# Expert weights of 18 of 25 row tiles carried in the scattered rows and applied in ScalarE's copy of an expert tile's result

## What the reference computes

```python
tokens = patches @ W.T + b;  h = concat(class, tokens * pos, txt)      # [16, 193, 128]
h = h + linear_attention(layernorm(h)) + depthwise_conv3(layernorm(h))
xt = layernorm(h)
_, idx = top_k(xt @ gate_w.T + biases, 2)          # which two experts
topv, _ = top_k(xt @ gate_w.T, 2)                  # the two best raw scores
p = sigmoid(topv);  p = p / p.sum(-1, keepdims=True)
y[e] = (silu(xt @ w1[e]) * (xt @ w3[e])) @ w2[e]   # for the chosen e
out = h + p[0] * y[idx[0]] + p[1] * y[idx[1]] + shared(xt)
```

## Time and profile before

| | us |
|---|---|
| median of 3 runs | 252.32 (251.96 to 253.23) |
| the profiled execution: its own time, its span | 254.19, 252.3 |
| busy in the span: PE, DVE, ACT, POOL | 223.3, 190.1, 155.8, 114.7 |

### The profile page before, as it was taken

The page is one execution under the profiler, slowest core; times in us unless marked ns, Lnnn a source line. Parts: engine busy times, 40 slices in busy tenths (PEclk is TensorE's granted clock), DMA queues, the critical chain, the costliest instruction groups (busy, mean ns, idle before and its releaser), DMA issues.

```text
span 252.3 us, 5578 instructions
## 1 busy us (share of the span) xinstructions
PE 223.3 (89%) x1477; PEld 191.5 (76%) x1485; DVE 190.1 (75%) x741; ACT 155.8 (62%) x438; POOL 114.7 (45%) x122
## 2 busy tenths in 40 slices
PE   3888879999899999988989979999999999999930
PEld 2768779989798989766576657888888888887720
DVE  3548896999999999988986778666666666665892
ACT  3056575676876867849863266666666666666390
POOL 1400000084837483803667703666666666666400
PEclk9999995999999999979999999999999999999995
DMA  6999981060607010100113331423332232329666
GB/s 189 353 360 355 328 315 62 0 232 26 233 24 243 22 56 22 42 10 13 55 42 93 79 83 34 115 62 100 92 89 81 84 94 83 90 81 275 159 157 190
DMA packets 31565, 31.68 MB, mean 126 GB/s; under 512 B 4338, under 2 KB 27419, under 8 KB 30768
## 3 DMA queue, kind: packets, MB, share of 16 engines
q1 hardware_dynamic: 27240, 24.57, 32.5%
q0 software_dynamic: 3392, 6.36, 7.7%
q10 hardware_dynamic: 904, 0.41, 0.6%
HBM read 22.80 MB, written 9.03 MB: 126 GB/s over the span
## 4 chain that ended last, share of the span: by engine, by line
PE 60%; DVE 24%; ACT 6%; issue 4%; DMA 2%; SPq 1%; DVEq 0%; ACTq 0%
PE bank L1621 15%; PE bank L1641 10%; PE bank L1630 5%; PE bank L1539 3%; PE bank L1333 3%; PE bank L1524 3%; PE bank L1527 3%; DMA cst<-in_consts 2%; DVE st L842 2%; PE bank L1610 2%; PE bank L1402 2%; PE bank L1416 2%; DVE sh_h L1103 2%; DVE att L908 2%; DVE att L899 2%
## 5 line engine op out<-in xcount | busy, mean ns | idle before, releaser
L813 POOL DMA_INDIRECT xs_dram<-xd,pos_i x50 | 55.4, 1109 | 69.7 <-DVE pos_i L1002 56.9
L824 POOL DMA_INDIRECT y_dram<-att,goal x56 | 55.1, 985 | 37.3 <-ACT att L749 37.0
L1333 PE MATMUL bank<-wt,xp_both 128*128 128x128 f32 x288 | 39.6, 290 | 5.7 <-DMA xp_both<-in_patches 5.4
L1333 PEld LDWEIGHTS bank<-wt,xp_both 128*128 128x128 f32 x288 | 37.3, 202 | 7.3 <-DMA xp_both<-in_patches 5.9
L735 ACT ACTIVATE att<-bank 128x256 f32<-128x256 f32 x56 | 21.5, 384 | 24.4 <-PE bank L1621 24.0
L1240 DVE CAST xsT_h<-bank 128x128 fp32r<-128x128 f32 x56 | 16.3, 291 | 24.4 <-PE bank L1610 24.4
L1641 PE MATMUL bank<-w_sb,att 128*128 x224 | 34.7, 277 | 0.0
L1641 PEld LDWEIGHTS bank<-w_sb,att 128*128 128x128 f32 x224 | 29.4, 191 | 0.5 <-issue 0.2
L1621 PE MATMUL bank<-xp_both,xsT_h 128*128 x56 | 26.8, 479 | 0.8 <-DVE xsT_l L1242 0.8
L1253 DVE TENSOR_TENSOR att<-att,bank 128x256 f32<-128x256 f32 x56 | 23.0, 411 | 1.7 <-ACT att L735 1.7
L1621 PE MATMUL bank<-xp_both,xsT_l 128*128 x56 | 22.2, 396 | 0.0
(11 more groups left out here) (212 smaller groups left out, 498.7 us busy)
## 6 DMA issues: line engine op xcount, KB each, us to landing
xp_both<-in_patches SPq DMA_DIRECT2D x6, 1152.0 KB
xs_all<-xs_dram SPq DMA_DIRECT2D x56, 64.5 KB, 1.8
xd<-y_dram SPq DMA_DIRECT2D x8, 384.0 KB, 4.8
w<-in_w SPq DMA_DIRECT2D x2, 1024.0 KB, 11.3
y_dram<-att,goal POOLq DMA_INDIRECT x56, 2.3
xs_dram<-xd,pos_i POOLq DMA_INDIRECT x50
xp_both<-in_patches SPq DMA_DIRECT2D x1, 768.0 KB, 5.6
hrow<-in_txt SPq DMA_DIRECT2D x2, 384.0 KB, 6.9
```

The lines of the kernel that those rows point to most:

```text
L813: nc.gpsimd.indirect_dma_start(out=xs_dram[:, :], out_offset=bass.IndirectOffsetOnAxis(ap=pos_i[0:rows, j, k:k + 1], axis=0), in_=xd[0:row ...
L824: nc.gpsimd.indirect_dma_start(out=y_dram[:, :], out_offset=bass.IndirectOffsetOnAxis(ap=goal[u][:, 0:1].bitcast(I32), axis=0), in_=ys[u][ ...
L1333: M(ps[:, 0:D], xp[p][:, k, :], wt[:, k, :], start=(k == 0), stop=False)
```

## The change

For the groups 0 to 5 (EARLIER = 6, the tiles below FROM = 18) the weight of each copy is computed before the scatter and travels as a second word of the row (ROW = 130 instead of 129 floats). `positions` no longer sorts these tokens' positions; copy k is choice k. POOL puts the sort into the goal instead (`goals`: it adds or subtracts the size of a half where the first choice is the higher expert), and computes the weights (`shares`: ten POOL operations for a group with `goals`, eight of them followed by a wait for the operation itself, which `pool_chain` counts). ACT gives the exponentials (`chances`), waiting for POOL's `shares` of the group before. ACT's copy of an expert tile's result multiplies by the word. Tiles 18 to 24 (LATE = 7 of them) keep the old way, with word 1.0. In the tail DVE adds chunks 0 to 2 as they are, ACT multiplies tiles 18 to 23 of both halves (`late_results`), and the order of DVE's tail is another.

```diff
-                nc.scalar.copy(ys[buf][:], bank[6 + q][:, 0:D]).then_inc(ys_done[at], 1)
+                A(ys[buf][:], bank[6 + q][:, 0:D], ACT.Copy, scale=goal[buf][:, 1:2]).then_inc(ys_done[at], 1)
...
+            def chances(g):
+                act.wait_ge(both_done, g + 1)
+                after(act, pool_chain, WEIGHED * g)
+                A(odds[:], raw8[:, 3 * g:3 * g + 3, 0:2], ACT.Exp, scale=-1.0).then_inc(odds_done, 1)
...
                 by_turns(i)
+                if i >= 2:
+                    chances(i - 2)
                 exps_rest(i)
...
+            def goals(g):
+                at = slice(3 * g, 3 * g + 3)
+                pool.wait_ge(both_done, g + 1)
+                then_pool(nc.gpsimd.tensor_copy(chosen[:], ix8[:, at, 0:2]))
+                then_pool(nc.gpsimd.tensor_tensor(crossed[:], chosen[:, :, 0], chosen[:, :, 1], ALU.subtract))
+                then_pool(nc.gpsimd.tensor_scalar(apart[:], crossed[:], 0.0, float(NID), ALU.is_gt, ALU.mult))
+                nc.gpsimd.tensor_tensor(xd[:, at, 0, D].bitcast(I32), ids[:, at, 0], apart[:], ALU.add)
+                nc.gpsimd.tensor_tensor(xd[:, at, 1, D].bitcast(I32), ids[:, at, 1], apart[:], ALU.subtract)
+            def shares(g):
+                at = slice(3 * g, 3 * g + 3)
+                pool.wait_ge(odds_done, g + 1)
+                then_pool(nc.gpsimd.tensor_scalar(odds[:], odds[:], 1.0, None, ALU.add))
+                then_pool(nc.gpsimd.tensor_tensor(odds[:], odds[:], minus[:].rearrange("p (t k) -> p t k", k=2), ALU.pow))
+                then_pool(nc.gpsimd.tensor_tensor(odds_sum[:], odds[:, :, 0], odds[:, :, 1], ALU.add))
+                then_pool(nc.gpsimd.tensor_tensor(odds_sum[:], odds_sum[:], minus[:, 0:3], ALU.pow))
+                then_pool(nc.gpsimd.tensor_tensor(xd[:, at, :, D + 1], odds[:], odds_sum[:].rearrange(
+                    "p (t o) -> p t o", o=1).broadcast_to([P, 3, 2]), ALU.mult))
             for g in range(G):
+                if g < EARLIER:
+                    goals(g)
+                    shares(g)
...
-                V.tensor_reduce(pos_2[:, a:b, :], prod[:, a:b], AX.X, ALU.add).then_inc(slots_done, 1)
-                dve.wait_ge(slots_done, g + 1)
-                    V.tensor_reduce(pos_i[:, a:b, 0], pos_2[:, a:b, :], AX.X, ALU.min)
-                    V.tensor_reduce(pos_i[:, a:b, 1], pos_2[:, a:b, :], AX.X, ALU.max).then_inc(pos_done, 1)
+                    if g < EARLIER:
+                        V.tensor_reduce(pos_i[:, a:b, :], prod[:, a:b], AX.X, ALU.add).then_inc(pos_done, 1)
...
-            then(V.tensor_tensor(swap[:], ix8[:, :, 0], ix8[:, :, 1], ALU.is_gt))
-            dve.wait_ge(raw_done, J)
+            then(V.tensor_tensor(swap[:], ix8[:, FROM:, 0], ix8[:, FROM:, 1], ALU.is_gt))
...
+            def add_results(c, k):
+                dve.wait_ge(y_loaded[k][c], 16)
...
+                    if b == CLS:
+                        dve.wait_ge(scaled, k + 1)
+                    last = V.tensor_tensor(hrow[:, a:b, :], hrow[:, a:b, :], y_rows[:, k, a:b, :], ALU.add)
```

More of the change, by code:

```diff
@@ L35 @@
 NID = J * P
+EARLIER = G - 2
+FROM = 3 * EARLIER
+LATE = J - FROM
 CAP = 3328
+WEIGHED = 8
 TILES = (2 * NTOK - E) // P + E
-ROW = D + 1
+ROW = D + 2
 BIG = 1 << 20
@@ L672, in _ @@
             rstd2(G - 2)
+            chances(G - 3)
             key_sums(G - 1)
@@ L759, in _, with late_results @@
             expert_steps(act, act_step, 2)
-            def second_results(c):
-                a = CHUNKS[c][0]
-                act.wait_ge(y_loaded[1][c], 16)
-                for j in range(a, weighed_by_act(c)):
-                    last = A(y_rows[:, 1, j, :], y_rows[:, 1, j, :], ACT.Copy, scale=weight[:, 1, j:j + 1])
+            def late_results(k):
+                c = len(CHUNKS) - 2
+                act.wait_ge(y_loaded[k][c], 16)
+                for j in range(FROM, CLS):
+                    last = A(y_rows[:, k, j, :], y_rows[:, k, j, :], ACT.Copy, scale=weight[:, k, j - FROM:j - FROM + 1])
                 last.then_inc(scaled, 1)
@@ L770, in _ @@
             shared_silu(EARLY + 1, 0)
+            late_results(0)
             shared_silu(EARLY + 1, 1)
-            second_results(0)
             shared_silu(EARLY + 2, 0)
             shared_silu(EARLY + 2, 1)
-            second_results(1)
-            for c in range(2, len(CHUNKS) - 1):
-                second_results(c)
+            late_results(1)
             for turn, c in list(enumerate(FINISHED))[2:]:
@@ L958, in raw_best @@
                 for j in tiles_of(g):
[L959 removed]
+                    V.max(raw8[:, j, :], sc[:, j, :])
             def choices(g):
@@ L1263, in _ @@
             expert_steps(dve, dve_step, 2)
-            def first_results(c):
+            def add_results(c, k):
                 a, b = CHUNKS[c]
                 rows = rows_of(a)
-                dve.wait_ge(y_loaded[0][c], 16)
-                for j in range(a, b):
+                dve.wait_ge(y_loaded[k][c], 16)
+                if k == 1:
+                    dve.wait_ge(fin_first, c + 1)
+                if a == CLS:
                     last = V.scalar_tensor_tensor(
-                        out=hrow[0:rows, j, :], in0=y_rows[0:rows, 0, j, :], scalar=weight[0:rows, 0, j:j + 1],
-                        in1=hrow[0:rows, j, :], op0=ALU.mult, op1=ALU.add)
-                last.then_inc(fin_first, 1)
@@ L1276, in all_results @@
-            def all_results(c):
-                a, b = CHUNKS[c]
-                m = weighed_by_act(c)
-                rows = rows_of(a)
-                dve.wait_ge(fin_first, c + 1)
-                dve.wait_ge(y_loaded[1][c], 16)
-                for j in range(m, b):
-                    last = V.scalar_tensor_tensor(
-                        out=hrow[0:rows, j, :], in0=y_rows[0:rows, 1, j, :], scalar=weight[0:rows, 1, j:j + 1],
-                        in1=hrow[0:rows, j, :], op0=ALU.mult, op1=ALU.add)
-                if m > a:
-                    dve.wait_ge(scaled, c + 1)
-                    last = V.tensor_tensor(hrow[:, a:m, :], hrow[:, a:m, :], y_rows[:, 1, a:m, :], ALU.add)
-                last.then_inc(fin_done, 1)
+                        out=hrow[0:rows, CLS, :], in0=y_rows[0:rows, k, CLS, :], scalar=weight[0:rows, k, CLS - FROM:LATE],
@@ L1292, in _ @@
+                        in1=hrow[0:rows, CLS, :], op0=ALU.mult, op1=ALU.add)
+                else:
+                    if b == CLS:
+                        dve.wait_ge(scaled, k + 1)
+                    last = V.tensor_tensor(hrow[:, a:b, :], hrow[:, a:b, :], y_rows[:, k, a:b, :], ALU.add)
+                last.then_inc(fin_done if k else fin_first, 1)
             dve.wait_ge(weight_done, 1)
             dve.wait_ge(sh_add, EARLY)
-            first_results(0)
-            first_results(1)
+            add_results(0, 0)
```

74 lines of the change are left out of this document (45 added, 29 removed).

## The result

The changed kernel takes 257.24 us (median of 4 runs, 256.76 to 258.37), the kernel before 252.60 beside it (251.96 to 253.23). The ratio is 1.019 with a 95% interval of 1.0146 to 1.0234. The prediction, 251.3 us with a range of 249.6 to 252.9, was wrong: the time lies 4.3 us above the upper end.

A forecast was written before the change was run, and what follows sets the result against it. PE bounds the kernel (60% of the chain); DVE's work counts only where PE waits. Loop -1.05, hits +0.4, ordering -0.2, tail -0.2 give -1.05 us: from 252.32 to 251.3 us, range 249.6 to 252.9.

The forecast's parts named there:

- the price of `goals` and `shares`: POOL, ahead of six groups' scatters: ten operations take 2.8 us (0 to 5.8), covered by 3.67 us of idle time.
- a scatter that starts a few us late costs nothing by itself: POOL's scatters: no engine waits before the first expert tile; idle times of 9.75 and 2.30 us precede groups 5 and 6.
- rival (3): ACT waits for POOL at `chances` from some 5.4 us a group on: some 254 us; chance 0.05.
- clock rival: TensorE's lowered clock at 107 to 117 us: shifted work escapes it, 1.7 us won, 249.6 us; chance 0.07.
- The loop: Attention loop: shorter `positions` lets DVE's turn start 0.25 us earlier in four iterations, 0.05 in a fifth: 1.05 us gained.
- ScalarE's exponentials and scaled copies: ACT: exponentials of some 0.2 us hide in a 0.7 us loop wait; scaled copies fit ACT's free time in the experts.
- The ordering by slot: DVE behind the loop: five operations shrink to 7 or 14 columns while PE idles 0.45 us; 0.2 us gained.
- The tail: Output end: first chunk's add ends at 242.7 instead of 242.88, SP's 7.59 us of issues follow; 0.2 us gained.
- the first `TENSOR_TENSOR`'s load of code: POOL's start: one code load, up to 8 us less the ten operations free; at about 6 us POOL starts some 1 us late.
- The 0.4 us for hits on DVE: Loop: POOL's operations beside DVE's turns delay DVE by one hit of 0.1 us in four iterations, 0.4 us lost.
- rival (2): POOL's work beside all three turns: three hits of 0.22 us in five iterations, 254.2 us; chance 0.08.
- rival (1): POOL's work fits ahead of DVE's turns in the loop, so 0.4 us is not lost: 250.9 us; chance 0.26.

The follow-up runs named there:

- goals only: Kernel before plus five POOL goal operations, first six groups unsorted on DVE, weights and tail as before: 253.52 us; second run 251.41 us.
- no powers: Changed kernel with POOL's two powers per group replaced by multiplications over the same tiles, so weights are wrong: 250.19 us, ratio 0.993.
- one power: Changed kernel with the same weights from one power instead of two, nine POOL operations per group: 250.87 us, ratio 0.990.
- before with ten operations: Kernel before plus the ten POOL operations per group for six groups, on tiles nobody reads: 256.69 us, ratio 1.019.

## Why the prediction was wrong

**The step that failed** is the price of `goals` and `shares`: "I take 2.8, ten copies end to end, since operands of 3 to 6 columns are smaller still and the waits make up for it". Measured were 5.5 us, beside the upper bound of 5.8 that the same paragraph gives, and 0.55 us an operation, which the prediction itself named as a sign of being wrong. The count of operations and waits was priced rightly (2.61 us with multiplications); that two of the ten are powers was not priced at all. A copy says nothing of a power: 1.37 us for six columns, 0.86 for three when nothing runs beside it. With these the ten take 4.46 us, as in group 5, which lies behind the loop. The rest, 1.0 us a group on average, is POOL held up: 0.1 by a wait for ScalarE in group 0, and 0.9 by VectorE, as shown below under the hits. Over groups 1 to 4 that is 5.2 us (5.76 + 6.61 + 5.09 + 5.57 less 4 x 4.46), as much as TensorE's added wait. So the powers' own time may not have been enough: (4.46 - 3.1) x 6 = 8 us is an estimate that stays inside the idle time of 12. No run has powers without the hold-ups, so how the two share the loss is not shown; without the powers there are neither.

**The step that hid it**: "a scatter that starts a few us late costs nothing by itself". It holds for one late scatter, but the lag adds up. The prediction's own numbers, 9 us of scatters and a threshold of 3.1 us, give (5.5 - 3.1) x 6 = 14 us for six groups against idle times of 9.75 + 2.30 = 12 us; rival (3) worked out this lag for ScalarE's queue and did not carry it on to the last scatter, where the first expert tile waits. The lag can be read against the second run of goals only, whose first scatter starts at the same time (48.30 us): at group 4 the changed kernel is 11.8 us behind (107.99 against 96.22), and at the last scatter 4.6 are left (145.94 against 141.31, in an execution with the low clock at 128 to 132 us). ScalarE never waited for POOL.

**A term that was missing** is what the wait does to TensorE: the low clock behind 5.85 us of idle time. The changed kernel's experts and tail are 1.6 us longer than those without powers, and with the clock kept up 2.2 us of the median came back. The prediction had a clock rival for a stretch where TensorE was idle already, not for one that the change would make idle.

**What was right.** The loop: 0.26 us less from reduction to turn (0.25 taken) and iterations shorter by as much, though only 0.6 to 0.9 of the 1.05 us show in the times of goals only. ScalarE's exponentials and scaled copies cost nothing: the copy grew from 0.27 to 0.37 us, but no powers and one power, which hold it, have no longer rest of the span than before. The ordering by slot: 0.2 us taken, and PE's wait behind it (L1577, L1539 before) fell from 0.45 to 0.30 us. The tail: gain 0.2 us taken, and the rest of the span went from 103.3 before to 103.0 to 103.2 in the versions whose experts began without a wait; the wait of 1.83 us ahead of the 16-column products was named, with 1.7. No delay by the first `TENSOR_TENSOR`'s load of code is to be seen: in the first group L830 starts at 42.09 and L831, behind the load's rows at 42.2 and 42.3, at 42.36 us, as far apart as in later groups.

**The 0.4 us for hits on DVE** did not come, nor the larger price of rival (2). The turns beside POOL's operations still take 0.95 us; the ones held up were POOL's. POOL after, beside the turns from 71.64 us on (the first is shown above), and the other two turns:

```profile
71.68 1.04 POOL L832 TENSOR_SCALAR apart<-crossed 128x3 int32<-128x3 f32 x1
72.80 0.71 POOL L833 TENSOR_TENSOR xd<-dest_sb,apart 128x3 int32<-128x3 int32 x1
...
73.65 1.00 POOL L840 TENSOR_SCALAR odds<-odds 128x6 f32<-128x6 f32 x1
```

```profile
72.51 0.95 DVE L947 TENSOR_TENSOR att<-att,cosx 128x768 f32<-128x768 f32 x1
...
73.58 0.95 DVE L954 TENSOR_TENSOR att<-att 128x768 f32<-128x768 f32 x1
```

Alone, L840 takes 0.25 us; begun just behind a turn's start, it ends some 0.1 us after the turn's end, as L832 and L833 do. The Trainium skill (SBUF — State Buffer, "Who interferes with whom") says that issue order, not the shape of an operation, decides which of the two blocks; the trace agrees, with POOL the later one in these rows. The other order is not seen to hold VectorE up: a turn that started at 106.36 us, beside a power that ran from 105.56 to 107.16, took 0.95 us too.

So without the powers rival (1), 250.9 us, would have been the case: the runs without powers and without shares measured 250.2 and 250.9, and at like clocks 1.6 and 1.5 us less than before, where rival (1) says 1.45.

## What to carry to other kernels

Work that moves to an engine with idle time is paid from the idle time of each period: if work and period differ by 3 us, four periods use up 12 us of slack behind the loop, so follow the lag to the last iteration and to the first reader. Price each operation by its own kind; a row of another operation bounds the issue and the waits, not the arithmetic. Where two engines can hold each other up, price it for both: here the later one, POOL, paid. And where a new wait falls on TensorE, add the clock behind it to its price.

## What the runs showed of the hardware

- A power on GpSimd took 1.37 us for six columns and 0.86 for three, where adds and multiplications of the same tiles take 0.19 to 0.21. The Trainium skill (GPSIMD Engine Reference, "3.1 Elementwise — side-by-side cycle accounting") puts GpSimd's elementwise work at about 2.6 cycles per element, measured on an add. These rows show a factor of four to seven between operations of one shape, so the figure for an add does not price a power.
- TensorE's clock fell to the lower level in a gap of 5.85 us without work and stayed there for the first 5 us of the experts; it fell in a gap of 3.04 us, too (before with ten operations: 0.57 from 151 to 156 us), and with 8 matmuls in the gap it did not.
- The low clock also comes and goes between executions of one and the same kernel, at 38 to 45 us, 107 to 113 and (in five profiled executions) between 128 and 134. Together with other such stretches it moves a run by some 4 us: the kernel before took 250.46 us at a mean clock of 0.988 and 254.97 at 0.968.
